# The bias of finished node tiles: added by ScalarE after VectorE's node sums, instead of by VectorE before them

## The reference

```python
e = edge_feats @ W_e + b_e                    # 200000 x 128
m = relu(e + x[src])
agg = segment_sum(m, dst, num_segments=6250)
h = agg + (1.0 + eps) * x
z = h @ W1 + b1                               # 6250 x 256
mu, var = mean(z, axis=0), mean((z - mu) ** 2, axis=0)
z = relu((z - mu) * rsqrt(var + 1e-5) * gamma + beta)
x = layernorm(x + z @ W2 + b2)
# ... then three GCN layers on x over the same edges, residual, layernorm
```

## Time and profile before

| | |
|---|---|
| runs of the kernel before | 2935.84, 2937.82, 2938.24 us; median 2937.82 |
| profiled execution, device time | 2933.97 us |
| its span, first to last instruction | 2932.2 us |
| granted TensorE clock, mean of the span | 0.888 |
| busy: PE, DVE, ACT, POOL | 2321.6, 2448.0, 1586.2, 1544.9 us |
| gathers by GpSimd (L852) | 1563 instructions, 1487.7 us busy, 473.9 us between them |
| finishing a tile by VectorE (L1456) | 45 instructions, 9.5 + 9.2 us |

### The profile page before, as it was taken

How to read it: one execution, slowest core, us unless ns; L and a number is a source line. 1 busy time by engine, 2 the same in 40 slices (tenths; PEclk the granted TensorE clock), 3 DMA queues, 4 the chain that set the end, 5 groups by cost and what they waited for, 6 DMA issues and landing times.

```text
span 2932.2 us, 43637 instructions
## 1 busy us (share of the span) xinstructions
PE 2321.6 (79%) x13267; PEld 1956.6 (67%) x13397; DVE 2448.0 (83%) x4293; ACT 1586.2 (54%) x2879; POOL 1544.9 (53%) x1688
## 2 busy tenths in 40 slices
PE   4677767776776767777777777777999999999998
PEld 3566656565665656666666665667788888888887
DVE  8999999899999999999999999996898844455554
ACT  5555555555555555555555555556555554455444
POOL 7777777777777777777777777762000000000111
PEclk8888888888888888888888888888999999999999
DMA  6445444444444444444444444445333333333432
GB/s 208 123 123 180 130 133 127 129 134 127 130 134 127 130 132 128 130 132 128 130 134 126 130 134 127 131 121 192 129 129 150 130 129 129 151 130 147 156 150 89
DMA packets 157965, 397.80 MB, mean 136 GB/s; under 512 B 37021, under 2 KB 100709, under 8 KB 152102
## 3 DMA queue, kind: packets, MB, share of 16 engines
q1 hardware_dynamic: 104854, 278.06, 26.4%
q0 software_dynamic: 51008, 105.74, 14.9%
q10 hardware_dynamic: 1872, 11.13, 1.0%
HBM read 289.99 MB, written 104.80 MB: 135 GB/s over the span
## 4 chain that ended last, share of the span: by engine, by line
POOL 44%; PE 30%; issue 16%; DVE 6%; DMA 2%; ACT 1%; SPq 0%; ACTq 0%; DVEq 0%; POOLq 0%
POOL work L852 44%; PE psE L1246 14%; PE psA L1246 13%; DVE z L1420 2%; DMA acc<-in_x_cols 1%; PE psA L1186 1%; DVE work L1428 1%; DVE work L1402 1%; DVE work L1427 1%; PE psA L1166 1%; ACT wide L1004 0%; PE psA L1114 0%; DMA work<-in_x_flat,idx 0%; PE psE L474 0%; DVE onehot L1408 0%
## 5 line engine op out<-in xcount | busy, mean ns | idle before, releaser
L852 POOL DMA_INDIRECT work<-in_x_flat,idx x1563 | 1487.7, 952 | 479.4 <-issue 473.9
L474 PE MATMUL psE<-we,work 128*128 128x256 f32 x1564 | 597.2, 522 | 207.1 <-DVE work L1402 189.7
L1420 DVE TENSOR_SCALAR z<-iota_r,key,scale 128x490 bf16<-128x490 f16 x1563 | 713.8, 520 | 0.5
L922 ACT ACTIVATE z<-psA 128x490 int32 x392 | 223.6, 571 | 708.6 <-PE psA L1114 700.3
L474 PEld LDWEIGHTS psE<-we,work 128*128 128x128 f32 x1564 | 422.9, 270 | 118.3 <-issue 36.5
L930 ACT ACTIVATE z<-iota_c,low 128x128 bf16<-128x128 f16 x1563 | 475.4, 389 | 0.0
L1246 PE MATMUL psE<-wide,halves 128*128 128x500 f32 (+1 forms) x2058 | 449.5, 376 | 5.8 <-ACT halves L1037 5.4
L1004 ACT ACTIVATE wide<-counts 128x1500 fp32r<-128x1500 uint8 (+2 forms) x182 | 273.7, 1504 | 281.4 <-PE psE L1246 139.9
L471 PEld LDWEIGHTS psE<-edge_bias,ones_b 128*128 128x128 bf16 x391 | 45.0, 115 | 561.3 <-issue 443.9
L1246 PEld LDWEIGHTS psE<-wide,halves 128*128 128x128 f32 x2058 | 364.9, 189 | 74.8 <-issue 7.0
L1602 DVE CAST wide<-counts 128x2000 fp32r<-128x2000 uint8 (+1 forms) x172 | 202.0, 1174 | 248.9 <-PE psA L1246 132.1
(11 more groups left out here) (195 smaller groups left out, 2360.5 us busy)
## 6 DMA issues: line engine op xcount, KB each, us to landing
counts<-adjacency SPq DMA_DIRECT2D x35, 3062.5 KB, 9.9
adjacency<-work SPq DMA_DIRECT2D x392, 245.0 KB
work<-in_edge_cols SPq DMA_DIRECT2D x196, 256.0 KB
work<-in_x_flat,idx POOLq DMA_INDIRECT x1563
counts<-adjacency SPq DMA_DIRECT2D x4, 1592.5 KB, 6.2
acc<-in_x_cols ACTq DMA_DIRECT2D x1, 3136.0 KB, 24.4
xn<-in_x_rows SPq DMA_DIRECT2D x1, 3136.0 KB, 13.2
acc<-degree_scratch ACTq DMA_DIRECT2D x1, 3136.0 KB, 16.0
```

Source lines behind the costliest of these rows:

```text
L474: mm = pe.matmul(psE0[0:n, 2 * q:2 * q + 2, :].rearrange("p j f -> p (j f)"), eaT[:, slot, q, 0:n], we[:, :], start=False, stop=True, skip ...
L852: gp.indirect_dma_start(gath[:, g % R, j, :], None, x_flat[:, :], bass.IndirectOffsetOnAxis(ap=idx[:, g, j:j + 1], axis=0)).then_inc(rows_ ...
L922: act.activation(taken[:, w % TAKEN, :, :], ring[:, bass.ds(at, 2 * HC)].rearrange("p (a n) -> p a n", a=ODD), ACT.Copy).then_inc(evac_ok, 1)
L1420: ve.tensor_scalar(hot[:, k % RB, :], iota_r[:, :, 0:2 * HC // ODD], key[:, k:k + 1], scale[:, k:k + 1], ALU.is_equal, ALU.mult).then_inc( ...
```

## The change

`finish_tile` moves from VectorE to ScalarE. VectorE's one instruction (128x256, both halves of the 256 first-layer values) becomes two ScalarE instructions (128x128 each, Identity with the bias as an operand). ScalarE runs them in turn s = g+1 of its loop, behind `low_hots` and ahead of the second `evacuate`, and waits for `win_added` g+1: VectorE's add of the same window, which reads the same bank, comes first now. TensorE's `window(g+2)`, which writes to this bank next, waits for both halves (`z_ok`). The counts of `z_ok` double. In the general path, which runs only when the input breaks an assumption on the window's width, SyncE and VectorE also wait for all of `z_ok`; the input here does not take that path.

```diff
 # ScalarE
+            def finish_tile(g, t):
+                act.wait_ge(win_added, g + 1)
+                act.wait_ge(deg_out, 16 * (t + 1))
+                for h in range(2):
+                    act.activation(acc[:, h, P * t:P * t + P], zwins[g % 2][:, h, :], ACT.Identity, bias=cols[:, h:h + 1]
+                                   ).then_inc(z_ok, 1)
...
                 if s + 3 < G:
                     low_hots(s + 3)
+                if s - 1 in ride:
+                    finish_tile(s - 1, ride[s - 1])
                 evacuate(row + 1, at[1])
 # TensorE, window(s)
+                if s - 2 in ride:
+                    pe.wait_ge(z_ok, 2 * (ride[s - 2] + 1))
 # VectorE
-            def finish_tile(g, t):
-                tile = slice(P * t, P * t + P)
-                if t == 0:
-                    ve.wait_ge(cols_par_in, 16)
-                ve.wait_ge(win_mm, g + 1)
-                ve.wait_ge(deg_out, 16 * (t + 1))
-                ve.tensor_tensor(acc[:, :, tile], zwins[g % 2], cols[:, 0:2].unsqueeze(2).to_broadcast([P, 2, P]), ALU.add
-                                 ).then_inc(z_ok, 1)
...
-                ve.wait_ge(z_ok, hi // P)
+                ve.wait_ge(z_ok, 2 * (hi // P))
...
-                if g in ride:
-                    finish_tile(g, ride[g])
                 add_window(g, at)
```

More of the change, by code:

```diff
@@ L508, in general_sum_sp @@
             sp.wait_ge(win_added, G)
+            sp.wait_ge(z_ok, 2 * NR)
             sp.dma_start(acc[:, 0, 0:NP], x_cols[:, :]).then_inc(sem_s["cols"], 16)
@@ L560, in general_sum_ve @@
             ve.wait_ge(deg_out, 16 * (NR + 1))
+            ve.wait_ge(z_ok, 2 * NR)
             ve.memset(acc[:, 1, :], 0.0).then_inc(sem_s["zero"], 1)
```

## The result

| | before | after |
|---|---|---|
| median, 12 runs each | 2939.01 us (2935.84 to 2940.77) | 2945.36 us (2942.36 to 2948.17) |
| ratio after/before, 95% interval | | 1.0021 (1.0013 to 1.0029) |
| profiled execution / its span | 2933.97 / 2932.2 us | 2942.36 / 2940.5 us |

The change costs about 6 us. The forecast was 2938.2 us with a range up to 2942.6, and gave "slower" 5%. Run again among the experiments it came out at 1.0017 (1.0008 to 1.0026), +5.1 us. So the loss is real and small, 5 to 6 us.

The account below looks back on a forecast made before the run. GpSimd's gathers were taken to pace the first stage, TensorE the second. The first three parts gave 0 and the stage's end +0.4 us, on a median of 2937.82: forecast 2938.2 us, range 2933.4 to 2942.6.

Parts of the forecast that it names:

- What bounds the kernel, and how far GpSimd is ahead: First stage: GpSimd's gathers set the pace, one each 1.2485 us, with a lead of 16.6 us at least.
- Part 1: VectorE loses 45 instructions, 18.7 us of its time; 44 lie where it idles for rows: saved 0.
- Part 2: ScalarE gains 90 instructions, 0.75 us a tile, which fit into its idle time: cost 0.
- Part 3: TensorE's windows start about 4 us late waiting for ScalarE; idle time before edge products and the gathers' lead cover it: 0.
- the prediction's own example, group 157: Its window starts 4.25 us later and ends at 1611.3; the edge product behind it is 0.5 us late.
- Part 4: End of the first stage: window 194 starts 1.2 us later, VectorE's last window add slips; +0.4 us, bounds -0.4 to +1.4.
- The Sum: Whole kernel: all terms together add 0.4 us, profiled execution 2934.4 us, median forecast 2938.2 us.
- The one for the late windows: First stage: TensorE's low clock makes lateness exceed the lead, about 3001 us, or 2945 if only last steps; together 5%.
- VectorE is the bound: First stage: VectorE sets the pace, so its freed 18.7 us count fully, 2919.1 us; with the port rival together 4%.
- the shared port: First stage: VectorE's tile adds lengthen gathers beside them by some tenths through an SBUF port; with the VectorE-bound rival 4%.
- A clock well below 0.84 in 400:1950: First stage: a granted clock falling well below 0.84 there would show the forecast wrong.
- VectorE's wait for an edge product: First stage: VectorE waiting for edge products in turns of finished tiles would show the forecast wrong.

Follow-up runs that it names:

- lean kernels: Changed kernel with a window waiting for `z_ok` in place of `win_added`, so TensorE has 45 wait instructions fewer; alone 1.0007, with further edits 1.0002 to 1.0007.
- r2_lean: Changed kernel, windows behind finished tiles waiting for ScalarE's reads alone, so 45 fewer wait instructions on TensorE; 2936.92 us, ratio 1.0007 to the kernel before.
- r3_lean_last2_ve: Against `r2_lean`, the tiles of groups 190 and 192 are finished by VectorE as before; 2936.00 us, ratio 1.0003 to the kernel before.
- r1_before: The kernel before run once more, nothing changed; 2935.87 us, ratio 0.9996.
- r1_after: The changed kernel run once more, nothing else changed; 2941.78 us, ratio 1.0017 to the kernel before.
- lean with 45 empty instructions: `r2_lean` with 45 empty semaphore instructions added to TensorE's program, on the slower chip; 3314.31 us, ratio 1.0021 to the kernel before.

## Why the prediction failed, by its own steps

**What bounds the kernel, and how far GpSimd is ahead: right.** GpSimd waits for nobody after the change, and leaving all finishes out is worth nothing.

**Part 1, VectorE's 45 instructions at 0: right.** As evidence it named a wait for rows that grows by 18 us. It grew by 10 (114.5 to 124.8), and by 12 to 13 with no finish at all, but hardly in the lean kernels (115.8 in `r2_lean`, 115.1 in `r3_lean_last2_ve`), so this sign was too weak to be read: VectorE's whole busy time in 400:1950 fell by 11 to 15 us in these kernels, and part of the idle time went into short waits for others.

**Part 2, ScalarE's 90 instructions at 0: right, the size a little off.** Two take 0.62 us, where 0.75 was taken: the lower bound from eight in a row (0.61) was the nearer one. One of them lasts 0.355 us. The estimate from the Trainium skill (ScalarE: Activation LUTs, Rules for kernel authors), 0.3 us and 0.83 ns an element, is 0.41 us; the measurement decides.

**Part 3, the late windows at 0: right in the sum, too rosy in the cover.** The waits were 3.9 us as worked out. TensorE's wait before edge products fell by more than the windows took. The trace of before lacks 130 matmul records of its first stage, so here are `r1_before` and `r1_after`, which lack none: in each the wait in 400:1950, and the busy time there as in the earlier trace rows.

```profile
PE psE L471 <- DVE work L1402: 410.1, 155, 4.9
...
400.00:1950.00 1550.00, 1141.55 (x7147) 943.79 (x7147) 1429.29 (x2544) 847.02 (x1858) 1171.84 (x1241) 0.84 0.44 130
```
```profile
PE psE L471 <- DVE work L1415: 219.1, 89, 4.6
...
400.00:1950.00 1550.00, 1164.07 (x7147) 981.85 (x7147) 1415.58 (x2502) 866.00 (x1945) 1171.92 (x1241) 0.82 0.44 130
```

191.0 us less, of which 163.4 moved to the windows; TensorE was busy 22.5 us longer, since products behind a long wait ran at the low level. The cover was computed at the speeds of before, and in the prediction's own example, group 157, it did not hold. Kernel after:

```profile
1615.10 1.19 PE L1109 MATMUL psA<-acc,w 128*128 128x128 f32 x4 [3.89 <-ACT acc L942]
...
1616.09 3.53 PE L1111 MATMUL psA<-onehot,work 128*128 128x72 f32 x16
...
1624.05 1.22 DVE L1415 TENSOR_TENSOR work<-psE,work 128x1024 f32<-128x1024 f32 x1 [2.25 <-PE psE L474]
```

The window's 16 products took 3.53 us, where they took 1.90 before, and VectorE waited 2.25 us for the edge product behind them: the sign that the prediction itself had named. The gathers' lead was least behind this window, 11.1 us where the least was 16.3 before. So the gathers did not wait, and 43 late windows cost nothing that can be measured.

**Part 4, the end of the stage: the term was mis-sized.** +0.4 us, with 1.4 as the upper bound; the runs say about 2, though no interval excludes 1.4. It started from window 194 alone and let the turn before it stand as in the earlier trace rows. But window 192 is late too, by 3.89 us and at half clock, and it lies ahead of edge product 194 and of window 193, for which VectorE then waits. Part 3 counted this very window among the 44 that have cover; the cover of a window so near to the end is used up once more, behind the last gather, where nothing idles.

**A term was missing, and it is the larger one: about 3 us of the 6.** Part 2 counted ScalarE's added instructions and Part 3 the added waits' time; no step counted the 45 instructions that the waits add to TensorE's program. Their own time is small (lean with 45 empty instructions is level with the kernel after), but they shift a branch and its target against the blocks in which instructions are loaded. The order's row with four waits on one matmul and `z_ok` among them had the information: 45 x one instruction, ahead of a branch. The Sum should have had a line for it with 0 as one end and a fetch as the other. Before, the trace had a price for a fetch, far from the place: TensorE's branch at the end of the program takes 3.65 us (3.88 after), with an instruction load that starts 0.94 us into it and ends 1.5 us ahead of its end; the one behind the first stage takes 0.37.

**The rivals.** The one for the late windows gave 2945 us if the last steps are hit, at a part of 5%. The time was met, but by two mechanisms of which only the smaller is that one. "VectorE is the bound" and the shared port are out.

**The sign of a wrong forecast.** A clock well below 0.84 in 400:1950 was named as one. It fell to 0.82 and was not the cause: with the tile ahead of `low_hots` it was 0.84 again and the time the same. VectorE's wait for an edge product was named too; it came once in the stage (2.25 us), without a measurable cost.

## What to carry to other kernels

When an edit adds waits, count the instructions that they become, and look at the next taken branch of that engine: pad the program with a few empty instructions to see whether its place matters before believing in a mechanism. Where one engine paces a stage, as the gathers do here, work moved between two others brought nothing; what part of its price could be seen in the stage was paid in the last two or three turns, around and behind the pacing engine's last instruction. Walk those turns one by one, the one before the last included. A saving should first be bounded by leaving the work out: here that gave 0.9997 (0.9988 to 1.0006), so the move could win next to nothing.

## What the runs showed of the hardware

- **A branch of TensorE costs 0.37 us or 2.3 to 3.6 us**, by where it lies in the program. Adding 20 instructions ahead of it left it cheap, 40 and 45 made it dear, 256 cheap again. In the seven dear cases a 16384-byte instruction load starts between 0.25 us ahead of the branch and 1.03 us into it, the branch ends 1.3 to 1.5 us behind the load's end, and the products behind the pause mostly run at the low level (2.94 to 3.61 us for 1.88).
- **An empty semaphore instruction** took TensorE 0.15 us in a row of them at the start of its program: 211 end at 32.96 us and put the first matmul off from 14.44 to 33.17 us, of which 3.2 us reached the gathers. 45 of them end at 7.48 us, while TensorE waits for its inputs anyway (first matmul at 14.53 us, against 14.58 without them).
- **A read of 128x128 from PSUM with a bias by ScalarE** takes 355 ns, two in a row 0.62 us from the first one's start to the second one's end.
- **One chip of those used was 12.6% slower** on the kernel before (3306.74 us for about 2936), with pauses of TensorE between count products of up to 2.0 us that name no releaser. The instruction loads themselves took as long there as elsewhere (medians 0.98 to 1.03 us there, 0.98 to 1.11 on the others). What holds TensorE up there stays open.
